# ViT tower with a top-2 mixture of experts: three of eight late shared blocks worked in halves between the routed units, and the low halves of the rows made on VectorE

## The chip, the cores and the metric

One core of one Trainium2 chip (trn2) runs the kernel. The metric is the device time of one execution in microseconds (us), all stages included. Engines are named as in the profile: PE is TensorE, DVE VectorE, ACT ScalarE, POOL GpSimd, SP SyncE, whose queue issues most transfers.

## What is computed

64 images of 3x224x224 become 197 tokens each of width 192. The reference, cut to what matters (x is the layer-normed h where the last line calls the feed-forward part):

```
h = tokens(images)                          # 16x16 patches, real FFT, projection
h = h + causal_conv(layernorm(h))           # a kernel of 512 taps for each channel
probs = softmax(x @ router_w); gates, idx = top_k(probs, 2)      # 8 experts
expert_out = (silu(x @ w_gate[e]) * (x @ w_up[e])) @ w_down[e]   # 192 -> 192 -> 192
routed = sum of the two chosen experts, by gate
shared = (silu(x @ ws_gate) * (x @ ws_up)) @ ws_down             # 192 -> 768 -> 192
alpha  = sigmoid(x @ sg_w + sg_b)
h = h + alpha * shared + (1 - alpha) * routed
```

## The kernel before

The program runs in stages with a barrier between each two: `embed` (tokens), `mix` (the convolution), then three stages of the feed-forward part, which the change touches. All products of these three are made of 16-bit high and low parts, so that each product is three to five matmuls.

**Shared stage** (`shared_expert`, from 330 us). The 12608 tokens are 25 blocks of `BT` = 512 (the last has 384). A block's shared expert is `NSH` = 6 chunks of 128 hidden units; a chunk is `up` on PE (5 + 5 matmuls of 512 columns), silu on ACT (L1233), `hidden` on DVE (hf, L1492), the high part on ACT (hh, L1239), `low` on DVE (hl, L1497) and `down` on PE (12 matmuls of 192 columns, L1160), which takes chunk c - 2 after `up` of chunk c. After six chunks `token_out` (L1504) adds a block to its sums in SBUF. Only the first `NOW` = 20 blocks get their chunks here, so 120 chunks; five blocks are left for the last stage.

In the same stage all 25 blocks must be prepared and routed. One *body* p of the schedule does that for a block while `PACE[p]` chunks are worked: 5, 5, 4, again and again, and 8 in the last. For each block: `add` on DVE (hin + yin, statistics, L1353 to L1367), `rstd` on POOL (the deviations, L1284 to L1291, ends in nb), `normal` and `x_high` on ACT (L1204, L1212: the normed rows and their high halves), `x_low` on POOL (L1296, L1297: their low halves), `transposes` on PE (L1110), `x_out` on ACT, `router` on PE, `logits` and top-2 on DVE, `ranks` on PE, `read_ranks` (L1406) and `slots` (its first is gb, its last L1442) on DVE, and `send` on POOL: two indirect DMAs (L1310) for each of four tiles scatter the rows to the list of their expert in DRAM. Before the first send of a block POOL runs one tiny operation, carry (L1308).

The order is written out by hand, one program for each engine, with semaphores. In body p POOL does send 0 and 1 of block p, `rstd` of block p + 2, send 2, `x_low` of p + 2, send 3. ACT does `normal` and `x_high` of block p + 1 in the first step of body p, after silu and before the silu of the next step. `ranks` and `slots` of block p come in the second step, or in the third where the body before had only four chunks:

```
def turn(p):
    return 2 if p and PACE[p - 1] == 4 else 1
```

In the last body, the fourth step also makes the table of the units (`unit_table`, L1454 to L1484, on DVE), after which SP writes fill rows behind each expert's list (L1096).

**Routed stage** (`routed_experts`, from 776 us). The lists are worked in units of 512 rows of one expert, here 52; the first `STRAIGHT` = 48 are written out, the rest run in a loop. A unit is 15 matmuls of 512 columns (`up`, L1652) and 20 of 192 (`down`, L1668), taken one unit later; the hidden values go through silu and parts on ACT and DVE (L1783 to L1791), `meta` and `y_out` on DVE (L1772) and ACT (L1691) write the gated result into one of two buffers y, and POOL sends it in four indirect DMAs (L1726) to DRAM. `y_out` of unit i waits until the sends of unit i - 2, which used the same buffer, have landed.

**Last stage** (`finish`, from 1161 us). The chunks of the five late blocks are worked as in the shared stage, in 30 steps (L1874, L1888), while all results are loaded, summed and stored.

The prepared rows of a late block stay in a ring of `XR` = 8 buffers xt until its chunks are done.

## Time and profile before

| what | us |
|---|---|
| median of 3 runs | 1275.32 (1271.84 to 1276.77) |
| the profiled execution, its own time | 1265.87 |
| its span, first to last instruction | 1264.0 |
| mean granted TensorE clock, share of full speed | 0.944 |
| busy: PE, DVE, ACT, POOL | 1044.1, 867.9, 537.2, 648.7 |
| shared stage, from its first silu to the barrier behind it | 330 to 776 |
| routed stage | 776 to 1161 |
| last stage | 1161 to 1264 |

Times in rows are us from the start of the span. "Busy" is the union of an engine's instructions; an engine with a lower share can still be the one that the others wait for. In a timeline a row is start, duration, engine, line, operation, out<-in, and in brackets the idle time before it with what ended it; "remote" is a semaphore of a DMA.

### The profile page before, as it was taken

How to read it: one execution, taken by the hardware profiler on the slowest of the kernel's cores; microseconds unless marked ns; L12 is line 12 of the kernel's file. 1: busy time of each engine (PE TensorE's matmuls, PEld its weight loads, DVE VectorE, ACT ScalarE, POOL GpSimd, SP SyncE). 2: the span in 40 equal slices, each digit the busy share in tenths (PEclk: the TensorE clock that was granted, in tenths of full speed). 3: DMA queues.
4: the chain of work that ended last, by engine and by line, in shares of the span. 5: the costliest groups of instructions: out<-in, count | busy, mean ns of one | idle time of the engine just before them, and what ended most of it. 6: DMA issues, size and time to landing. Idle time of an engine off the chain costs nothing. (4 is left out here: it accounts for less than half of the span.)

```text
span 1264.0 us, 24364 instructions
## 1 busy us (share of the span) xinstructions
PE 1044.1 (83%) x7867; PEld 719.3 (57%) x7868; DVE 867.9 (69%) x2637; ACT 537.2 (42%) x1023; POOL 648.7 (51%) x682
## 2 busy tenths in 40 slices
PE   5978997784699998999999996877778877773997
PEld 5867886683366655656666653444444444441555
DVE  6999776322487888978878763665665656651998
ACT  1234534222455565655555532444444444431332
POOL 0134412000377776777777760566666666643543
PEclk9988999787699999999999997999999899986999
DMA  8767786867994435443333126545545455333997
GB/s 295 241 231 262 238 261 157 208 137 172 200 210 137 118 92 133 135 116 96 99 102 93 52 81 175 121 102 127 121 98 126 105 118 126 87 77 105 308 305 239
DMA packets 285967, 196.08 MB, mean 155 GB/s; under 512 B 178840, under 2 KB 264602, under 8 KB 285590
## 3 DMA queue, kind: packets, MB, share of 16 engines
q1 hardware_dynamic: 251152, 142.46, 43.7%
q0 software_dynamic: 19488, 39.17, 9.1%
q10 hardware_dynamic: 15206, 12.93, 4.0%
q8 instruction: 66, 1.08, 0.4%
q14 instruction: 55, 0.45, 0.1%
HBM read 100.52 MB, written 74.65 MB: 139 GB/s over the span
## 5 line engine op out<-in xcount | busy, mean ns | idle before, releaser
L1726 POOL DMA_INDIRECT parts<-unit_yu,unit_token x208 | 217.5, 1046 | 69.9 <-issue 62.1
L1310 POOL DMA_INDIRECT routed<-rows_w,slot x198 | 215.8, 1090 | 65.6 <-issue 65.6
L1160 PE MATMUL pso<-ffn_w_hi,hh 128*128 128x192 f16 x480 | 119.3, 248 | 23.9 <-DVE hl L1497 17.6
L1492 DVE SCALAR_TENSOR_TENSOR hf<-psu,sg 128x512 f32<-128x512 f32 x120 | 82.9, 690 | 81.2 <-ACT sg L1233 39.6
L1233 ACT ACTIVATE sg<-psg 128x512 f32<-128x512 f32 x120 | 71.9, 599 | 142.8 <-PE psg L1145 96.0
L454 POOL TENSOR_TENSOR e_rs<-e_ve,mhalf 98x8 f32<-98x8 f32 x16 | 49.8, 3113 | 139.2 <-DVE e_ve L692 132.5
L1160 PE MATMUL pso<-ffn_w_hi,hl 128*128 128x192 f16 x480 | 119.0, 248 | 0.0
L1160 PE MATMUL pso<-ffn_w_lo,hh 128*128 128x192 f16 x480 | 119.0, 248 | 0.0
L1145 PE MATMUL psg<-xt,ffn_w_hi 128*128 128x512 f16 x360 | 118.5, 384 | 0.0
L1145 PE MATMUL psu<-xt,ffn_w_hi 128*128 128x512 f16 x360 | 117.9, 382 | 0.0
L1652 PE MATMUL u_gate<-unit_xtu,ffn_w_hi 128*128 128x512 f16 x156 | 55.6, 413 | 60.8 <-issue 35.1
L524 PE MATMUL ps<-w,area 128*98 128x192 f32 x528 | 100.6, 335 | 0.0
L402 ACT ACTIVATE u<-spare,e_nb,e_rs 98x192 f32<-98x192 f32 x124 | 56.1, 535 | 92.3 <-POOL e_nb L456 73.3
L1145 PE MATMUL psg<-xt,ffn_w_lo 128*128 128x512 f16 x240 | 92.1, 384 | 0.0
L1145 PE MATMUL psu<-xt,ffn_w_lo 128*128 128x512 f16 x240 | 91.7, 382 | 0.0
L1691 ACT ACTIVATE unit_yu<-u_out,unit_gates 128x192 f32<-128x192 f32 x104 | 38.1, 417 | 125.8 <-remote 78.3
L1497 DVE TENSOR_TENSOR hl<-hf,hh 128x512 f16<-128x512 f32 x120 | 90.7, 756 | 0.3 <-ACT hh L1239 0.3
L524 PEld LDWEIGHTS ps<-w,area 128*98 128x98 f32 x528 | 83.3, 169 | 5.3
L1783 DVE SCALAR_TENSOR_TENSOR unit_h<-u_up,stage 128x512 f32<-128x512 f32 x52 | 36.0, 692 | 60.9 <-remote 21.3
L1239 ACT CAST hh<-hf 128x512 f16<-128x512 f32 x120 | 73.7, 614 | 7.1 <-DVE hf L1492 4.9
L1921 POOL TENSOR_TENSOR end_part<-end_part 128x768 f32<-128x768 f32 (+1 forms) x25 | 47.4, 1899 | 55.8 <-DMA end_part<-parts 55.8
L1668 PE MATMUL u_out<-ffn_w_hi,unit_h0h 128*128 x208 | 51.8, 249 | 25.9 <-DVE unit_yu L1772 25.9
(245 smaller groups left out, 2806.9 us busy)
## 6 DMA issues: line engine op xcount, KB each, us to landing
end_part<-parts SPq DMA_DIRECT2D x48, 384.0 KB, 5.6
area<-in_xa_dram SPq DMA_DIRECT2D x33, 392.0 KB, 5.1
area<-in_xb_dram SPq DMA_DIRECT2D x33, 392.0 KB, 6.0
resid<-spare ACTq DMA_DIRECT2D x32, 294.0 KB
hin<-resid SPq DMA_DIRECT2D x24, 384.0 KB
yin<-mixed SPq DMA_DIRECT2D x96, 96.0 KB
spare<-in_xa_dram SPq DMA_DIRECT2D x15, 392.0 KB, 6.3
spare<-in_xb_dram SPq DMA_DIRECT2D x15, 392.0 KB, 7.4
```

The costliest lines, as they stand in the source:

```text
L402: last = nc.scalar.activation(u[0:HALF, n % 2, GI * g + n // 2], h[g % NH][:, n // 2, n % 2], ACT.Identity, bias=nb[g % NH][:, n], scale=r ...
L524: nc.tensor.matmul(out, xa[(C * g + c) % NSLOT][:, t], w32[:, c], start=(plain and c == 0 and k == 0), stop=False, skip_group_check=True)
L1145: last = nc.tensor.matmul(ps[:, m % 2], wt[:, k, cols], xt[b % XR][:, x], start=(a == 0), stop=(a == 4))
L1160: last = nc.tensor.matmul(o, hx[m % 2][:, ts], wd[k][:, m], start=(a == 0 and m == 0 and t % 2 == 0), stop=(a == 2 and m == NSH - 1), skip ...
L1233: nc.scalar.activation(sg[c % 2][:], psg[:, c % 2], ACT.Silu, scale=1.0 / SCALE).then_inc(s["sg_ready"], 1)
L1239: nc.scalar.copy(hh[c % 2][:], hf[c % 2][:]).then_inc(s["hh_ready"], 1)
L1310: nc.gpsimd.indirect_dma_start(out=routed[:, :], out_offset=bass.IndirectOffsetOnAxis(ap=slot[q][:, k, t:t + 1], axis=0), in_=rows_w[q][:, ...
L1492: nc.vector.scalar_tensor_tensor(out=hf[i][:], in0=psu[:, i], scalar=1.0 / SCALE, in1=sg[i][:], op0=ALU.mult, op1=ALU.mult).then_inc(s["hf ...
L1497: nc.vector.tensor_tensor(hl[c % 2][:], hf[c % 2][:], hh[c % 2][:], ALU.subtract).then_inc(s["hl_ready"], 1)
L1652: last = nc.tensor.matmul(ps[:], w[part][:, bass.ds(col + off, 128)], x[:, c], start=(m == 0), stop=(m == 4))
L1668: last = nc.tensor.matmul(o, h[q][:, k * 128:(k + 1) * 128], w[part][:, bass.ds(col + off, D)], start=(m == 0 and k % 2 == 0), stop=(m == ...
L1726: nc.gpsimd.indirect_dma_start(out=parts[:, :], out_offset=bass.IndirectOffsetOnAxis(ap=token[q][:, k:k + 1], axis=0), in_=y[q][:, k, :], ...
```

## The change

**The tables.** Eight blocks are late (`NLATE` = 8), so that only 17 blocks get their chunks in the shared stage: 102 chunks. `PACE` is 4 for each of the 24 bodies and 6 for the last. The number of bodies, and of blocks to be prepared and routed, is as before. `turn` is not edited, but with every body at 4 it gives 2 for all bodies but the first. The ring xt gets a ninth buffer, in the SBUF of `area`.

**The guests.** Three of the eight late blocks (17 to 19) are worked in the routed stage, in halves of 256 tokens: 3 blocks x 2 halves x 6 = 36 half chunks. Units 0 to 46 take one each, but for every fourth (3, 7, ...). A half chunk is 10 matmuls of 256 columns behind the unit's `up`, and 6 of 192 behind its `down` in the next unit; one silu and one copy on ACT; `hf` and `hl` on DVE, and two additions to the sums after each sixth. The last stage keeps five blocks and its 30 steps.

**The low halves.** `x_low` leaves POOL and becomes two operations of DVE, in the second step of a body.

```diff
@@ constants
-NLATE = 5
+NLATE = 8
+HOSTED = 3
 NOW = NBLK - NLATE
-PACE = [5, 5, 4] * ((NBLK - 1) // 3) + [8]
-XR = 8
+LATE = NOW + HOSTED
+PACE = [4] * (NBLK - 1) + [6]
+XR = 9
...
+HALVES = 2 * HOSTED
+GUESTS = NSH * HALVES
+GUEST_OF = {i: n for n, i in enumerate([i for i in range(STRAIGHT - 1) if i % 4 != 3][:GUESTS])}
+HB = BT // 2
@@ shared_expert, ScalarE
                 if b >= XR:
                     act.wait_ge(s["u_ps"], NSH * (b - XR + 1))
+                if b == XR - 1:
+                    act.wait_ge(s["area_out"], 64)
@@ shared_expert, GpSimd
-            def x_low(b, nt):
-                x = xs[b % NR]
-                pool.wait_ge(s["xhi_ready"], b + 1)
-                nc.gpsimd.tensor_tensor(x[:, 0:nt, D:D + 64], xn[:, 0:nt, 128:D], x[:, 0:nt, 128:D], ALU.subtract)
-                nc.gpsimd.tensor_tensor(x[:, 0:nt, D + 64:XW], xn[:, 0:nt, 0:128], x[:, 0:nt, 0:128],
-                                        ALU.subtract).then_inc(s["xlo_ready"], 1)
...
                 send(p, 2)
-                if a < NBLK:
-                    x_low(a, tiles(a))
                 if tiles(p) == NT:
                     send(p, 3)
@@ shared_expert, VectorE
+            def x_low(b, nt):
+                x = xs[b % NR]
+                dve.wait_ge(s["xhi_ready"], b + 1)
+                nc.vector.tensor_tensor(x[:, 0:nt, D:D + 64], xn[:, 0:nt, 128:D], x[:, 0:nt, 128:D], ALU.subtract)
+                nc.vector.tensor_tensor(x[:, 0:nt, D + 64:XW], xn[:, 0:nt, 0:128], x[:, 0:nt, 0:128],
+                                        ALU.subtract).then_inc(s["xlo_ready"], 1)
...
                     if c:
                         low(c - 1)
+                    if i == 1 and r < NBLK:
+                        x_low(r, tiles(r))
                     if c % NSH == 1 and c > NSH:
                         token_out(c // NSH - 1)
@@ routed_experts, TensorE
+            def guest_up(j):
+                b, half, m = guest_place(j)
+                cols, ts = slice(m * 128, (m + 1) * 128), slice(half * HB, (half + 1) * HB)
+                if j >= 2:
+                    pe.wait_ge(late["hf_ready"], j - 1)
+                for k in range(2):
+                    prods = ((wa[0], 0), (wa[1], 0), (wa[0], 2), (wb[0], 1), (wb[1], 1))
+                    for a, (wt, x) in enumerate(prods):
+                        last = nc.tensor.matmul(gps[:, j % 2, k * HB:(k + 1) * HB], wt[:, k, cols],
+                                                t["xt"][b % XR][:, x, ts], start=(a == 0), stop=(a == 4))
+                last.then_inc(late["g_ps"], 1)
...
             def body(i, q, k, landed):
                 up(i, k, landed)
+                if guest(i) is not None:
+                    guest_up(guest(i))
                 if not (isinstance(i, int) and i == 0):
                     down(i - 1, 1 - q)
+                if isinstance(i, int) and guest(i - 1) is not None:
+                    guest_down(guest(i - 1))
@@ routed_experts, ScalarE
                 nc.scalar.copy(h1s[q][S], h1[q][S]).then_inc(s["h1h_ready"], 1)
+                j = guest(i)
+                if j is not None:
+                    act.wait_ge(late["g_ps"], j + 1)
...
+                    nc.scalar.activation(sgx[j % 2], gps[:, j % 2, 0:HB], ACT.Silu,
+                                         scale=1.0 / SCALE).then_inc(late["sg_ready"], 1)
                 if not (isinstance(i, int) and i == 0):
                     y_out(i - 1, 1 - q)
+                if j is not None:
+                    act.wait_ge(late["hf_ready"], j + 1)
...
+                    nc.scalar.copy(hhx[j % 2][:], hfx[j % 2]).then_inc(late["hh_ready"], 1)
@@ routed_experts, VectorE
+                if isinstance(i, int) and guest(i - 2) is not None:
+                    guest_out(guest(i - 2))
+                j = guest(i)
+                if j is not None:
...
+                    nc.vector.scalar_tensor_tensor(out=hfx[j % 2], in0=gps[:, j % 2, HB:2 * HB], scalar=1.0 / SCALE,
+                                                   in1=sgx[j % 2], op0=ALU.mult,
+                                                   op1=ALU.mult).then_inc(late["hf_ready"], 1)
                 if not (isinstance(i, int) and i == 0):
                     meta(i - 1, 1 - q)
                     y_out(i - 1, 1 - q)
+                if j is not None:
+                    dve.wait_ge(late["hh_ready"], j + 1)
+                    nc.vector.tensor_tensor(hlx[j % 2][:], hfx[j % 2], hhx[j % 2][:],
+                                            ALU.subtract).then_inc(late["hl_ready"], 1)
@@ finish
-        CHUNKS = NSH * NLATE
+        CHUNKS = NSH * (NLATE - HOSTED)
```

The order of the program shows three places.

DVE, shared stage, the steps two and three of a body whose `turn` is 2 (hf and hl are `hidden` and `low`; rank and base are `read_ranks`). Before, in body 3, which follows a body of four:

```order
L1492 SCALAR_TENSOR_TENSOR hf<-psu,sg 128x512
L1497 TENSOR_TENSOR hl<-hf,hh 128x512
L1492 SCALAR_TENSOR_TENSOR hf<-psu,sg 128x512
L1406 TENSOR_TENSOR rank<-psx,base 128x32
L1409 TENSOR_TENSOR base<-base,psx 128x8
L1497 TENSOR_TENSOR hl<-hf,hh 128x512
L1417 TENSOR_SCALAR gb<-th 128x8
```

Now, in body 2, the same place, and so in all bodies but the first:

```order
L1500 SCALAR_TENSOR_TENSOR hf<-psu,sg 128x512
L1505 TENSOR_TENSOR hl<-hf,hh 128x512
L1373 TENSOR_TENSOR rows_w<-xn,rows_w 128x4x64
L1374 TENSOR_TENSOR rows_w<-xn,rows_w 128x4x128
L1500 SCALAR_TENSOR_TENSOR hf<-psu,sg 128x512
L1414 TENSOR_TENSOR rank<-psx,base 128x32
L1417 TENSOR_TENSOR base<-base,psx 128x8
L1505 TENSOR_TENSOR hl<-hf,hh 128x512
L1425 TENSOR_SCALAR gb<-th 128x8
```

Two subtractions into rows_w (`x_low` of the next block) now stand between the `hl` of the second step and the `hf` of the third, ahead of `read_ranks` and `slots`.

POOL, shared stage, one body (carry, the sends, the deviations of the block two further on). Before:

```order
L1308 TENSOR_TENSOR carry<-eps 128x1
L1310 DMA routed<-rows_w,slot 106496x196 x4
L1284 TENSOR_TENSOR ve<-mv,eps 128x4
L1288 TENSOR_TENSOR rs<-ve,mhalf 128x4
L1291 TENSOR_TENSOR nb<-nm,rs 128x4
L1310 DMA routed<-rows_w,slot 106496x196 x2
L1296 TENSOR_TENSOR rows_w<-xn,rows_w 128x4x64
L1297 TENSOR_TENSOR rows_w<-xn,rows_w 128x4x128
L1310 DMA routed<-rows_w,slot 106496x196 x2
L1308 TENSOR_TENSOR carry<-eps 128x1
```

Now:

```order
L1313 TENSOR_TENSOR carry<-eps 128x1
L1315 DMA routed<-rows_w,slot 106496x196 x4
L1296 TENSOR_TENSOR ve<-mv,eps 128x4
L1300 TENSOR_TENSOR rs<-ve,mhalf 128x4
L1303 TENSOR_TENSOR nb<-nm,rs 128x4
L1315 DMA routed<-rows_w,slot 106496x196 x4
L1313 TENSOR_TENSOR carry<-eps 128x1
```

The four sends and the deviations stand as they did; the two subtractions are gone from between the last four sends.

PE, routed stage, from the end of a unit's `up` to the start of the `down` of the unit before it (u_short is the third group of `up`, u_out is `down`). Before:

```order
L1652 MATMUL u_short<-unit_xtu,ffn_w_hi 128x512
L1652 REGISTER_ALU
L1652 MATMUL u_short<-unit_xtu,ffn_w_lo 128x512
L1613 TENSOR_LOAD units
L1613 ISA x2
L1668 ISA
L1668 MATMUL u_out<-ffn_w_hi,unit_h0h 128x192
```

Now:

```order
L1708 MATMUL guest_up<-area,ffn_w_hi 128x256 x2
L1708 MATMUL guest_up<-area,ffn_w_lo 128x256
L1708 MATMUL guest_up<-area,ffn_w_hi 128x256
L1708 MATMUL guest_up<-area,ffn_w_lo 128x256
L1708 MATMUL guest_up<-area,ffn_w_hi 128x256 x2
L1708 MATMUL guest_up<-area,ffn_w_lo 128x256
L1631 TENSOR_LOAD units
L1631 ISA x2
L1695 ISA
L1695 MATMUL u_out<-ffn_w_hi,unit_h0h 128x192
```

Ten matmuls of 256 columns (the last five stand here) come between the two; `area` is the ninth buffer of the ring.

## Rows read from the trace of the kernel before

**Rows 1.** windows of the four late stretches (stretch, us, busy of each engine, PEclk, DMA, GB/s)

```profile
330.00:739.00 409.00, 390.98 (x3324) 250.42 (x3323) 326.88 (x1291) 227.45 (x422) 296.70 (x332) 0.99 0.44 115
739.00:776.00 37.00, 28.75 (x198) 18.10 (x196) 23.25 (x79) 9.77 (x18) 11.59 (x13) 0.91 0.50 159
776.00:1161.00 385.00, 281.64 (x1821) 166.31 (x1822) 214.87 (x520) 159.02 (x312) 228.20 (x262) 0.93 0.47 106
1161.00:1264.00 103.00, 93.76 (x642) 57.06 (x640) 86.71 (x104) 32.00 (x60) 47.43 (x25) 0.96 0.90 284
```

**Rows 2.** instructions of one tile: carry, one per block (min/median/max ns)

```profile
L1308 POOL TENSOR_TENSOR carry<-eps x25: 189/190/592, 340.7 to 750.3; 128x1 f32<-128x1 f32 x25
```

**Rows 3.** chain of waits, one step in the last stage (start us, us)

```profile
1214.33 1.08 PE end_gate L1874 x5
1215.40 1.08 PE end_up L1874 x5
1216.48 0.99 PE end_out L1888 x12
```

**Rows 4.** timeline of ScalarE in body 15, which follows a body of four

```profile
592.07 1.86 ACT L1204 ACTIVATE xn<-area,nb,rs 128x192 f32<-128x192 f32 x4 [3.01 <-POOL nb L1291]
...
594.70 0.59 ACT L1233 ACTIVATE sg<-psg 128x512 f32<-128x512 f32 x1
```

**Rows 5.** timelines of VectorE and TensorE in body 15

```profile
595.32 0.69 DVE L1492 SCALAR_TENSOR_TENSOR hf<-psu,sg 128x512 f32<-128x512 f32 x1 [2.84 <-PE psu L1145]
595.93 1.35 DVE L1497 TENSOR_TENSOR hl<-hf,hh 128x512 f16<-128x512 f32 x1
...
598.32 0.68 DVE L1497 TENSOR_TENSOR hl<-hf,hh 128x512 f16<-128x512 f32 x1
...
599.99 0.17 DVE L1442 CAST slot<-slotf 128x8 uint32<-128x8 f32 x1
...
597.34 0.26 PE L1160 MATMUL pso<-ffn_w_hi,hh 128*128 128x192 f16 x1 [1.92 <-DVE hl L1497]
```

**Rows 6.** timeline of GpSimd in body 18: carry, and nb four sends later

```profile
650.66 0.19 POOL L1308 TENSOR_TENSOR carry<-eps 128x1 f32<-128x1 f32 x1 [1.90 <-DVE slot L1442]
...
657.69 0.20 POOL L1291 TENSOR_TENSOR nb<-nm,rs 128x4 f32<-128x4 f32 x1
```

**Rows 7.** timelines of GpSimd and VectorE: a send beside a sum

```profile
633.89 1.53 POOL L1310 DMA_INDIRECT routed<-rows_w,slot  x1 [0.16 <-issue]
...
633.61 0.95 DVE L1353 TENSOR_TENSOR area<-hin,yin 128x768 f32<-128x768 f32 x1
```

**Rows 8.** timeline of GpSimd, nb of block 2; instructions of L1504

```profile
352.02 0.21 POOL L1291 TENSOR_TENSOR nb<-nm,rs 128x4 f32<-128x4 f32 x1
...
L1504 DVE SCALAR_TENSOR_TENSOR spare<-pso,alpha,spare x48: 402/408/414, 404.6 to 647.5; 128x192 f32<-128x192 f32 x48
```

**Rows 9.** timelines of GpSimd and of SyncE's queue at the stage's end

```profile
750.27 0.19 POOL L1308 TENSOR_TENSOR carry<-eps 128x1 f32<-128x1 f32 x1 [4.79 <-DVE slot L1442]
...
758.09 11.32 SPq L1096 DMA_DIRECT2D routed<-stage  x8
...
776.38 0.10 POOL L1731 MEMSET unit_const<- 128x1 f32 x1 [17.72 <-POOLq L930]
```

**Rows 10.** timeline of VectorE: results of three routed units, one after another

```profile
916.22 0.74 DVE L1772 TENSOR_SCALAR unit_yu<-u_out,unit_gates 128x192 f32<-128x192 f32 x2 [2.72 <-remote]
...
921.24 0.74 DVE L1772 TENSOR_SCALAR unit_yu<-u_out,unit_gates 128x192 f32<-128x192 f32 x2
...
929.77 0.74 DVE L1772 TENSOR_SCALAR unit_yu<-u_out,unit_gates 128x192 f32<-128x192 f32 x2 [2.67 <-remote]
```

**Rows 11.** timelines of GpSimd and TensorE beside them

```profile
917.20 0.19 POOL L1722 TENSOR_TENSOR unit_carry<-unit_const 128x1 f32<-128x1 f32 x1 [2.23 <-DVE unit_yu L1772]
...
922.11 0.98 POOL L1726 DMA_INDIRECT parts<-unit_yu,unit_token  x1 [0.30 <-DVE unit_yu L1772]
...
917.15 0.25 PE L1668 MATMUL u_out<-ffn_w_hi,unit_h0h 128*128 x1 [2.00 <-DVE unit_yu L1772]
```

More of the change, by code:

```diff
@@ L900, in feed_forward @@
              + [x[:, 0:HELD * D].rearrange("p (t d) -> p t d", d=D) for x in (spare, area)]}
+        late = {name: ctx.enter_context(nc.semaphore("e_" + name)) for name in
+                ("g_ps", "u_ps", "sg_ready", "hf_ready", "hh_ready", "hl_ready", "down_ps", "out_ready")}
         shared_expert(nc, io, t, spare, area, block_stored, y_stored, weights, resid, mixed, routed, out, consts)
-        routed_experts(nc, t, weights, routed, parts)
-        finish(nc, t, weights, parts, out)
+        routed_experts(nc, t, late, weights, routed, parts)
+        finish(nc, t, late, weights, parts, out)
 def tiles(b):
@@ L1523, in _ @@
             stage_low(2)
+            x_low(0, NT)
             stage_low(3)
@@ L1558, in _, with routed_experts @@
             token_out(NOW - 1)
-def routed_experts(nc, t, weights, routed, parts):
+def routed_experts(nc, t, late, weights, routed, parts):
     with ExitStack() as ctx:
@@ L1774, in y_out, with guest_out @@
                 last.then_inc(s["y_d"], 1)
+            def guest_out(j):
+                b, half, m = guest_place(j)
+                if m < NSH - 1:
+                    return
+                dve.wait_ge(late["down_ps"], j + 1)
+                for k in range(2):
+                    at = 2 * half + k
+                    sums = sums_of(t, b, NT)[:, at]
+                    last = nc.vector.scalar_tensor_tensor(
+                        out=sums, in0=gpo[:, k * D:(k + 1) * D], scalar=t["alpha"][b % XR][:, at:at + 1], in1=sums,
+                        op0=ALU.mult, op1=ALU.add)
+                last.then_inc(late["out_ready"], 1)
             dve.sem_inc(s["begun"], 1)
@@ L1964, in _ @@
                 if c % NSH == 1 and c > NSH:
-                    token_out(NOW + c // NSH - 1)
+                    token_out(LATE + c // NSH - 1)
                 elif c >= 2:
```

73 lines of the change are left out of this document (54 added, 19 removed).

## The prediction

> **What bounds the kernel now.** I read the windows of the late stretches first, then the timelines of one body of the shared stage, then those of one pair of routed units. The windows show TensorE (PE) busy for 391 of the 409 us of the 24 bodies, and for 282 of the 385 us of the routed stage, at 0.93 of its clock there [rows 1]. So the shared stage is bound by PE, the routed stage by something else, and the change carries PE work from the first to the second. That is its plain promise. A step of chunk work is 1.08 + 1.08 + 0.99 = 3.15 us of PE [rows 3]; the 112 steps in the bodies make 353 us, which leaves (391 - 353) / 24 = 1.6 us for the transposes, router and ranks of a block.
>
> What the reader is to see next is that a body is not only PE work. Every block passes once round a ring of engines, and POOL's carry marks the turns: 25 of them from 340.7 to 750.3, so 17.07 us for a block [rows 2]. PE needs (112 / 24) x 3.15 + 1.6 = 16.3 us of that.
>
> The ring is: nb on POOL, `normal` and `x_high` on ACT, silu, `hidden`, `low`, `read_ranks` and `slots` on DVE, carry and four sends on POOL, nb. With `turn` at 2 it has no slack across bodies: `slots` of block p + 1 stands behind the silu that stands behind `normal` of block p + 2, and nb of p + 3 stands behind the sends of p + 1. Body 15 shows its first part, since it follows a body of four: ACT sat 3.01 us until nb, began `normal` at 592.07, the next silu only at 594.70 [rows 4], and `slots` ended at 599.99 + 0.17 = 600.16 [rows 5]. PE itself stood 1.92 us behind `hl` there [rows 5]. The second part is 7.23 us in body 18, from carry at 650.66 to the end of nb at 657.89 [rows 6]. Before, only one body in three has this order, and the longer bodies give the loss back.
>
> In the routed stage `y_out` waits for a DMA ("remote") at every other unit: 2.72 us at 916.22 and 2.67 us at 929.77, not at 921.24 [rows 10]. The cycle is `y_out`, four sends on POOL (917.20 to 923.09), and some 6.7 us until the buffer is free: 13.55 us for two units. PE waits for it too, 2.00 us in the same place [rows 11].
>
> **The change, part by part.**
>
> *Fewer chunks in a body.* 18 steps x 3.15 = 56.7 us of PE work leave the shared stage. PE would need 4 x 3.15 + 1.6 = 14.2 us for a block. But the ring now holds in all bodies: 600.16 - 592.07 = 8.09 us from `normal` to the end of `slots`.
>
> *`x_low` on DVE.* It stands inside this ring, ahead of `slots`. No row shows it on DVE. The nearest is `hl`, which is a subtraction of the same kinds, 0.68 us for 512 columns [rows 5]; 256 + 512 columns are 1.0 us. Below, the second start hidden under the first leaves 0.8; above, 1.35, as `hl` took beside a POOL operation [rows 5]. I take 1.0. What goes is that very clash: `hl` takes 0.68 again, so -0.67. The first part of the ring is 8.09 + 1.0 - 0.67 = 8.4 us. Queued behind `x_low` on DVE are `hidden` of the third step, `read_ranks` and `slots`; POOL waits for these, PE for the rows. On POOL the removal gives nothing to the ring: the subtractions stood behind nb, and POOL has 8.4 us there for four sends (7.23 us hold four sends and nb).
>
> *Carry to nb.* 7.23 us when nothing meets it. `add` of the next block now follows `slots` at once on DVE, and a send beside that sum took 1.53 instead of 0.97 us [rows 7]. The first send starts 0.7 us behind carry, late in a sum of 0.95, and one later send may meet a `low`: I take 0.3 us for both, bounds 0 and 2 x 0.56. The turn is 8.4 + 0.1 (slots to carry) + 7.55 = 16.05 us, bounds 15.5 and 16.8.
>
> By the Trainium skill (SBUF — State Buffer, "SBUF: two separate sides") VectorE and GpSimd share one port pair as an exclusive lock: a VectorE operation with two SBUF inputs keeps out a GpSimd operation that reads SBUF until it ends. By that rule `x_low`, `hl` and the sum of `add` can each hold a send, and the send of rows 7, begun 0.28 us into the sum, would be held 0.67 us: 1.64 against 1.53 measured, so the trace agrees. It speaks against putting `x_low` on VectorE, and is the long-turn rival below.
>
> *`token_out`.* It is 4 x 0.41 us [rows 8], 1.35 us back to back. In 8 of the 24 turns (chunks 13, 25, ... 97) it stands between `x_low` and `slots`: +10.8 us.
>
> *Sum of the bodies.* nb of block 2 ends at 352.23 [rows 8]; it waits for loads that do not change. Carry of block 1 is then 352.23 + 8.4 + 0.15 = 360.8, carry of block 24 is 360.8 + 23 x 16.05 + 10.8 = 740.7, against 750.27 [rows 9]: **-9.6 us**. The other 47 us of PE work removed become waiting of PE.
>
> *The last body.* It has two steps fewer (6.3 us). SP's fill rows, hung on the table of units, run until 758.09 + 11.32 = 769.41, and the next stage begins at 776.38 [rows 9]. They start 1.35 us earlier after carry, since no `token_out` stands there now, but still have to land. So the stage ends about 750.27 - 740.7 earlier, plus a part of the 7.0 us behind the fill rows: bounds 0 and 6.3, I take **-4.8**.
>
> *Ninth buffer.* ACT waits once for stores that were issued in the third and fourth body, and once, for block 24, for one `up` more: nothing in the ring; 0 to 2 us, taken as 0.
>
> *Guests in the routed stage.* A half chunk is half of 2.16 and half of 0.99, 1.58 us of PE, 57 us in all. PE is busy 282 / 52 = 5.4 us for a unit; two units and 1.5 guests are 10.8 + 2.4 = 13.2 of the 13.55 us of the cycle. On DVE `hf` and `hl` of 256 columns are 0.35 us each, and now and then 0.8 us of sums, against waits of 2.7 us ahead of the result that is waited for. ACT has more room (159 of 385 busy). What hides them is the time in which sends land; the margin on PE is 0.35 us a pair. Not hidden is the start, where no send is yet under way: two guests ahead of the first `down` and a part of a third, 3 us. For half-clock stretches in which PE has no rest left I add 2: **+5**, bounds 0 and 15 (a quarter of the 57).
>
> *Last stage.* The same 30 steps and transfers (DMA share 0.90 [rows 1]): 0.
>
> **Sum.** -9.6 - 4.8 + 5 = -9.4 us. The profiled execution took 1265.87, so 1256.5; that execution lies 9.4 below the median of the runs, 1275.32. I take the difference to the median: **1266 us**. A measurement of this kernel can tell about 0.5%, 6.4 us, from no change.
>
> **The rivals.**
>
> *Ring as forecast:* turn 15.8 to 16.3, 1260 to 1272 us. For it: two of the three parts were read in bodies with this order. Chance 0.55, of which 0.38 faster, 0.17 same.
>
> *Short turn:* 15.5, because `x_low` overlaps and no send is met. 23 x -0.55 = -12.6: 1253 us. For it: 7.23 was measured. Against: body 18 had no `add` at its start. 0.15, faster.
>
> *Long turn:* two of the four sends meet a DVE operation with two inputs, turn 16.8, +17: 1283 us. For it: rows 7, and the skill's rule, which is the same mechanism. Against: only one sum lies near each carry. 0.12, half same, half slower.
>
> *Guests break the cycle of the results* (the other side): DVE does `hf`, now and then the sums, and `hl` around `y_out`, and PE has 0.35 us to spare. If the result comes later than the buffer by all of the guests' DVE time, 1.2 us in each of 24 cycles, +29 for the +5 (which it contains): 1290 us, slower. It decides where the wait before `y_out` falls under 1.2 us; before it was 2.7. 0.08.
>
> *No ring:* if `slots` did not stand behind nb, PE would bind, 14.2 us a turn and `token_out` beside it: carry of block 24 at 687.4, -62.9 - 4.8 + 5: 1213 us. For it: PE's share of 391 in 409 us. Against: rows 4 and 5. 0.05, faster. The last 0.05 is for what I don't see: 0.02 faster, 0.02 same, 0.01 slower.
>
> **How the numbers follow.** Faster by over 0.5% 0.60, within 0.25, slower 0.15. The range of 1248 to 1284 us takes in the forecast, both turns and the bounds of the tail; it leaves out the guests' rival, the kernel without a ring and a part of the rest, 0.18.
>
> **What would show it.** Carry: 25 rows from 340 to 741, 16.5 us apart on the whole, mostly released by `slots`. ACT: a wait for nb in nearly every body. PE: some 2 us behind `hl` or the transposes in each body, busy share of the bodies near 0.87 and not 0.95. `x_low` near 1.0 us. Routed stage: 390 us, PE busy near 340, "remote" still ahead of every other `y_out`. Wrong it is if carry comes less than 15.3 us apart on the whole (then no ring), if carry to nb is over 8 us (port), or if "remote" is gone and the routed stage is over 400 us.

## The result, and the profile after

The changed kernel takes **1292.07 us** (median of 4 runs, 1289.18 to 1293.85), the kernel before 1276.05 us beside it (median of 4, 1271.84 to 1279.71). The ratio is 1.0124, with a 95% interval of 1.0087 to 1.0162: slower by 1.2%, where 1266 us was forecast and 1284 was the upper end.

The profiled execution took 1291.38 us (span 1289.5), close to its median. That of before, 1265.87, lies 10.2 us under its median. So the traces stand 25.5 us apart, the medians 16.0; what follows divides up the 25.5.

The windows of the changed kernel's late stretches answer to [rows 1] (shared bodies, end of the shared stage, routed stage, last stage):

```profile
330.00:739.00 409.00, 354.38 (x2980) 224.18 (x2978) 308.24 (x1288) 210.53 (x391) 253.30 (x285) 0.97 0.42 113
739.00:780.00 41.00, 22.56 (x140) 13.91 (x139) 19.33 (x74) 6.46 (x12) 11.16 (x14) 0.78 0.53 159
780.00:1180.00 400.00, 337.14 (x2393) 217.60 (x2391) 245.57 (x604) 184.69 (x384) 220.69 (x260) 0.95 0.46 100
1180.00:1289.00 109.00, 93.58 (x642) 57.35 (x642) 79.63 (x104) 31.96 (x60) 46.45 (x25) 0.94 0.84 269
```

TensorE is as busy as the forecast wanted to see it, 354 of 409 us in the bodies (0.87) and 337 in the routed stage. What is wrong is the lengths. They stand in three rows of instructions by tile: carry, the first projection of the units, and the sends of the results:

```profile
L1313 POOL TENSOR_TENSOR carry<-eps x25: 189/832/835, 338.6 to 750.6; 128x1 f32<-128x1 f32 x25
L1679 PE MATMUL u_gate<-unit_xtu,ffn_w_hi x156: 379/379/634, 778.4 to 1157.5; 128*128 128x512 f16 x156
L1793 POOL DMA_INDIRECT parts<-unit_yu,unit_token x208: 969/977/1449, 794.5 to 1176.8; - x104
```

Carry of block 24 comes at 750.6, not at 740.7 as forecast, and not earlier than before [rows 2]. In the trace of before, units began at 780.7 and the last send at 1150.1. Against before:

| piece | before | after | difference | forecast |
|---|---|---|---|---|
| start to carry of block 24 | 750.3 | 750.6 | +0.3 | -9.6 |
| carry to the first unit | 30.4 | 27.8 | -2.6 | -4.8 |
| first unit to the start of the last send | 369.4 | 398.4 | +29.0 | +5 |
| from there to the end of the span | 113.9 | 112.7 | -1.2 | 0 |
| sum | 1264.0 | 1289.5 | +25.5 | -9.4 |

The medians differ by 9.5 us less than these traces. Which piece holds these 9.5 us isn't known; if all of them are in the routed stage, its growth on the median is 19.5 us and not 29.

**The ring, and what was left out of it.** A turn is the time from one block's carry to the next one's. The timeline of GpSimd and VectorE in two turns of the changed kernel, a late one and one of the eight between blocks 6 and 14:

```profile
666.31 0.83 POOL L1313 TENSOR_TENSOR carry<-eps 128x1 f32<-128x1 f32 x1 [2.50 <-DVE slot L1450]
673.74 0.20 POOL L1303 TENSOR_TENSOR nb<-nm,rs 128x4 f32<-128x4 f32 x1
678.55 0.42 DVE L1373 TENSOR_TENSOR rows_w<-xn,rows_w 128x256 f16<-128x256 f32 x1
678.88 0.69 DVE L1374 TENSOR_TENSOR rows_w<-xn,rows_w 128x512 f16<-128x512 f32 x1
682.32 0.83 POOL L1313 TENSOR_TENSOR carry<-eps 128x1 f32<-128x1 f32 x1 [2.50 <-DVE slot L1450]
...
460.05 0.83 POOL L1313 TENSOR_TENSOR carry<-eps 128x1 f32<-128x1 f32 x1 [3.51 <-DVE slot L1450]
467.47 0.20 POOL L1303 TENSOR_TENSOR nb<-nm,rs 128x4 f32<-128x4 f32 x1
468.67 1.35 DVE L1525 SCALAR_TENSOR_TENSOR ffn_w_lo<-stage,ffn_w_hi 128x1152 f16<-128x1152 f32 x1
473.25 0.42 DVE L1373 TENSOR_TENSOR rows_w<-xn,rows_w 128x256 f16<-128x256 f32 x1
477.02 0.83 POOL L1313 TENSOR_TENSOR carry<-eps 128x1 f32<-128x1 f32 x1 [3.52 <-DVE slot L1450]
```

The first turn is 16.01 us: 7.63 from carry to the end of nb, 8.38 from there to the next carry (forecast 7.55 and 8.5, turn 16.05). x_low is two instructions, 1.02 us from start to end, and 0.94 of it until the next can start. Of the six turns with token_out ahead of slot and no row of weights, three are 17.2 to 17.3 (forecast 17.4) and the others 17.8, 18.0 and 18.5. So the ring is as forecast in the plain turns. But the second turn is 16.97, because the row of 1.35 us stands in it, the low half of a staged piece of weights (`stage_low`). Eight turns have it; the six of them without token_out are 16.97 to 17.14, 0.9 to 1.1 us over 16.05, and all eight together are 6.7 us over the forecast's turns. No term of the forecast holds it, though it stood in the kernel's own order.

**The routed stage.** From the first unit to the last, before and after:

```profile
781.00:1131.00 350.00, 273.36 (x1768) 160.43 (x1767) 207.37 (x498) 154.51 (x302) 214.75 (x245) 0.96 0.50 112
```
```profile
780.00:1158.00 378.00, 329.05 (x2343) 212.73 (x2342) 238.40 (x582) 180.18 (x374) 208.31 (x245) 0.97 0.47 103
```

The guests add 55.7 us to TensorE's busy time. Its rest falls from 76.6 to 48.9 us, and the other 28 us make the stage longer.

VectorE's results, the last matmul of TensorE's second projection ahead of two of them, and sends (timelines of VectorE, TensorE and GpSimd; before, the same cycle is [rows 10, 11]):

```profile
797.81 0.25 PE L1695 MATMUL u_out<-ffn_w_lo,unit_h1s 128*128 x1
800.72 0.74 DVE L1839 TENSOR_SCALAR unit_yu<-u_out,unit_gates 128x192 f32<-128x192 f32 x2 [1.56 <-remote]
...
926.52 0.74 DVE L1839 TENSOR_SCALAR unit_yu<-u_out,unit_gates 128x192 f32<-128x192 f32 x2
932.73 0.97 POOL L1793 DMA_INDIRECT parts<-unit_yu,unit_token  x1 [1.90 <-remote]
934.01 1.07 POOL L1793 DMA_INDIRECT parts<-unit_yu,unit_token  x1 [0.30 <-issue]
939.77 0.25 PE L1695 MATMUL u_out<-ffn_w_lo,unit_h1s 128*128 x1
943.91 0.74 DVE L1839 TENSOR_SCALAR unit_yu<-u_out,unit_gates 128x192 f32<-128x192 f32 x2 [2.37 <-remote]
```

"remote" stands ahead of 20 results, for 32.8 us in all (before 23, 43.0). The word was read as the semaphore of a DMA, here as a send that has not landed, and that reading is wrong. The result at 800.72 is that of the second unit, the first to use its buffer: in the program it waits for no send, and the label is there all the same. What it does wait for is TensorE's signal that `down` is done, and this comes late: it is recorded at 800.70, where the last matmul ended at 798.06. The result at 943.91 is alike. Its buffer's last send (934.01) landed early: sixteen signals, those of a whole send, are recorded at 937.36 to 937.49. TensorE's last matmul for it ended at 940.02, and the signal came at 943.88. In all 20 cases, and in all 23 before, the last signal on record is TensorE's, 0.02 to 0.03 us ahead of the result. (Signal times are in the packed trace and in no view of it.)

Before, the result at 916.22 [rows 10] is the same case. The last matmul of its `down` and the last of the next unit's `up`:

```profile
910.51 0.25 PE L1668 MATMUL u_out<-ffn_w_lo,unit_h1s 128*128 x1
914.77 0.38 PE L1652 MATMUL u_short<-unit_xtu,ffn_w_lo 128*128 128x512 f16 x1
```

The signal of `down` is recorded at 916.19, 5.4 us after the end, and those of the three groups of `up` at 916.26, 916.33 and 916.40, though their last matmuls had ended at 912.99, 914.07 and 915.15.

Late signals are so common that they shape the stage: those of `down` come more than 0.3 us behind their last matmul in 27 of 49 units here, by 2.9 us in the median, and in 31 of 50 before, by 5.2. The send at 932.73 waited 1.90 us for one too, since the program lets it start on a signal of TensorE. From one result of a buffer to the next the mean is 14.8 us now and 13.6 before (units 2 to 47; the pair shown, 17.4, is one of the longest). The part up to the end of the fourth send is the same, 7.2 us, and the part behind it grew from 6.5 to 7.6. So the cycle got longer, but it isn't the landing of sends that closes it.

### The profile page after: what moved, and what is told of

Its sections match the earlier page's. It is cut to its first block and busy times, and to the rows that moved or that the text cites. A ratio compares the mean times of both kernels' runs of the same rounds, so it can differ in the third digit from the quotient of the medians.

```text
span 1289.5 us, 24848 instructions
## 1 busy us (share of the span) xinstructions
PE 1057.7 (82%) x8047; PEld 740.5 (57%) x8048; DVE 872.2 (68%) x2723; ACT 543.4 (42%) x1059; POOL 593.2 (46%) x632
## 2 busy tenths in 40 slices
DMA packets 285971, 196.13 MB, mean 152 GB/s; under 512 B 178840, under 2 KB 264602, under 8 KB 285590
## 5 line engine op out<-in xcount | busy, mean ns | idle before, releaser
L1170 PE MATMUL pso<-ffn_w_hi,hh 128*128 128x192 f16 x408 | 103.4, 254 | 55.8 <-DVE hl L1505 30.1
L1500 DVE SCALAR_TENSOR_TENSOR hf<-psu,sg 128x512 f32<-128x512 f32 x102 | 70.3, 690 | 90.6 <-ACT sg L1245 58.0
L1170 PE MATMUL pso<-ffn_w_hi,hl 128*128 128x192 f16 x408 | 103.4, 253 | 0.0
L1170 PE MATMUL pso<-ffn_w_lo,hh 128*128 128x192 f16 x408 | 103.3, 253 | 0.0
L1155 PE MATMUL psg<-xt,ffn_w_hi 128*128 128x512 f16 x288 | 97.2, 393 | 0.0
L1155 PE MATMUL psu<-xt,ffn_w_hi 128*128 128x512 f16 x288 | 94.7, 383 | 0.0
L1170 PEld LDWEIGHTS pso<-ffn_w_hi,hh 128*128 128x128 f16 x408 | 40.8, 100 | 78.1 <-DVE hl L1505 43.0
L1155 PE MATMUL psg<-xt,ffn_w_lo 128*128 128x512 f16 x192 | 75.3, 392 | 0.0
L1155 PE MATMUL psu<-xt,ffn_w_lo 128*128 128x512 f16 x192 | 73.3, 382 | 0.0
L1505 DVE TENSOR_TENSOR hl<-hf,hh 128x512 f16<-128x512 f32 x102 | 69.7, 684 | 1.4 <-ACT hh L1251 1.4
```

Source lines behind the costliest of these rows:

```text
L1155: last = nc.tensor.matmul(ps[:, m % 2], wt[:, k, cols], xt[b % XR][:, x], start=(a == 0), stop=(a == 4))
L1170: last = nc.tensor.matmul(o, hx[m % 2][:, ts], wd[k][:, m], start=(a == 0 and m == 0 and t % 2 == 0), stop=(a == 2 and m == NSH - 1), skip ...
L1500: nc.vector.scalar_tensor_tensor(out=hf[i][:], in0=psu[:, i], scalar=1.0 / SCALE, in1=sg[i][:], op0=ALU.mult, op1=ALU.mult).then_inc(s["hf ...
L1505: nc.vector.tensor_tensor(hl[c % 2][:], hf[c % 2][:], hh[c % 2][:], ALU.subtract).then_inc(s["hl_ready"], 1)
```

## The experiments

The kernel before takes 1193 to 1195 us on the chips of sets 1, 2, 4 and 5 below, and 1279 on that of set 3, which alone is like the case's own. Ratios are against the kernel before on the same chip. The expectations of set 1 name times of the case's chip, which are some 83 us longer.

The expectations speak of chips where sends land early or late. The traces don't bear that out: what differs is TensorE's signals. Those of `down` are late in 27 to 34 of some 50 units in each trace of the case's chip and of set 3, and in none of any trace of the other sets. Below, the chips are told apart by that.

### Set 1: where the loss is

**Guests left out** (e1), so that three blocks lack their shared part:

```
-HALVES = 2 * HOSTED
+HALVES = 0
```

> The change, with the 36 guests left out on all engines: the shared expert's part of three blocks is missing from the sums. The routed stage took 370 us from its first matmul to its last send before the change, 399 with it. Theory A (the guests cost this on their own): the stage is back at 370 to 372 us, 28 us below the change, about 1263 us. Rival (something else of the change slows the routed stage: the longer program, the ninth buffer, the state in which the shared stage leaves the queues): the stage stays above 385 us, over 1278.

1189.81 us, ratio 0.9981 (0.9970 to 0.9991).

**Guests on TensorE alone** (e2): all their matmuls, none of their waits, and nothing of them on ScalarE and VectorE.

```
-                if j >= 2:
-                    pe.wait_ge(late["hf_ready"], j - 1)
...
-                pe.wait_ge(late["hl_ready"], j + 1)
...
-                        last = nc.tensor.matmul(gpo[:, k * D:(k + 1) * D], hx[j % 2][:, k * 128:(k + 1) * 128],
+                        last = nc.tensor.matmul(gpo[:, k * D:(k + 1) * D], t["xt"][b % XR][:, a, k * 128:(k + 1) * 128],
```

> The guests as work of TensorE alone: all their matmuls at the same places, waiting for nothing (the second projection reads a fixed tile), no silu, hidden, high, low or sums for them; three blocks' shared part is missing. Theory A1 (TensorE's time is not hidden: 57 us of it, of which about half shows): 1285 to 1292 us, as the change. Theory A2 (what costs is the chain of the results, that is the guests' operations on VectorE and ScalarE ahead of the results, while TensorE's part fits into its waits): within 5 us of the kernel without guests, about 1265.

1213.63 us, 1.0158 (1.0138 to 1.0179).

**stage_low in the last step of the body** (e3):

```
-                    if i == 0 and p and staged_at(p - 1):
-                        stage_low(staged_at(p - 1))
...
+                    if i == 3 and staged_at(p):
+                        stage_low(staged_at(p))
```

> The change, with the low half of a staged weight piece (1.35 us on VectorE) made in the last step of the body in place of the first step of the next. Theory B (it stands in the ring of the blocks in the ten turns from 443 to 617 us and makes each 0.95 us longer, which the forecast left out): carry of block 24 comes 9 to 10 us earlier, at 741, and the time is 8 to 10 us below the change, 1283. Rival (the turns of 17 us have another cause, such as the DMA of the loads or TensorE's lateness): carry stays at 750, no change of the time.

1204.92 us, 1.0101 (1.0084 to 1.0117).

**Guests behind the results of their unit** (e4), in words, since the same lines only change place:

```
 PE:   up(i); -guest_up(j);  down(i - 1); guest_down(j of i - 1); +guest_up(j)
 ACT:  +high(j of i - 1); silus and highs of the unit; -silu(j); y_out(i - 1); +silu(j); -high(j)
 DVE:  +low(j of i - 1); the unit's four; -hidden(j); meta, y_out(i - 1); +hidden(j); -low(j)
```

> The change, with each guest moved behind the results of its unit: TensorE makes its first projection after the unit's second one, ScalarE and VectorE take silu and hidden after y_out, and high and low at the start of the next unit, where they wait for TensorE anyway. Nothing is left out. Theory A2 (what stands ahead of the results costs): the routed stage falls by 15 to 25 us, total 1268 to 1277. Theory A1 (TensorE's time itself shows): no more than 5 us, 1287 to 1292.

1212.64 us, 1.0169 (1.0149 to 1.0189).

### Set 2: control, x_low, and a shorter ring (the same chip as set 1)

> The change, unaltered, beside the kernel before on the chip of this set: the control for the others. The first set ran on a chip on which the kernel before takes 1193 us and not 1276. Theory C (what the sends take to land differs between chips, the rest of the change costs the same): 1.2 to 1.8% over the kernel before. Rival: the loss belongs to the first chip, under 0.5%.

1212.72 us, 1.0171 (1.0146 to 1.0196): the change loses on this chip too, and somewhat more. This is what e1 to e4 are to be held against.

**x_low back on GpSimd** (e6), as the kernel before has it, with all the rest of the change.

> The change, with the low halves of the rows back on GpSimd, behind the third pair of sends as before. Forecast's term (1.0 us in the ring for x_low, 0.67 given back because low no longer meets it): the turns without token_out or stage_low, 16.0 us, become 15.7, carry of block 24 some 8 us earlier, the time up to 8 us below the change. Rival (the port: on GpSimd it slows the VectorE operations and is slowed by them): turns of 16.0 or more, no gain.

1210.89 us, 1.0159 (1.0132 to 1.0185), no difference from e5. Most plain turns fell from 15.9 to 16.1 only to 15.8 to 16.0; carry of block 24 came at 739.5 against 741.8. The move of x_low is worth about nothing within the change.

**A shorter ring** (e7), again in words:

```
 DVE   -x_low(r) in step 1            +x_low(r) in step 2, behind slots
 PE    -transposes(p + 1) in step 2   +in step 3, behind down
 PE    -router(p + 1) in step 3       +router(p) in step 0 of the next body, behind up
 ACT   -x_out(r) in step 2            +in step 3
 DVE   stage_low as in e3
```

> The change, with stage_low in the last step, x_low behind slots, the transposes of the next block behind the second projection of the last step, and its router behind the first projection of the next body. Theory B (ring: 7.6 us from carry to nb, 8.4 from nb to carry of which x_low is 1.0): turns of 15.0 us without token_out, 16.3 with it, carry of block 24 at 338 + 25 + 23 x 15.4 = 718 to 722, the time 25 to 30 us below the change. Rival (TensorE binds at 14.2 us plus what its records don't show): turns of 16, no more than the 9 us of stage_low.

**1183.32 us, 0.9920 (0.9894 to 0.9946)**: 29.4 us below the change and 0.8% below the kernel before.

> The kernel before, for its profile on the chip of this set. Theory C: its turns are 17.1 us as on the first chip, its unit takes 5.6 us where the sends land sooner, and no result waits for a DMA.

1193.84 us, one run, for its trace.

What the sets 1 and 2 show of the shared stage is in the rows of carry, of e3, e5 and e7 (instructions by tile, each of its own kernel):

```profile
L1313 POOL TENSOR_TENSOR carry<-eps x25: 188/830/834, 337.0 to 736.3; 128x1 f32<-128x1 f32 x25
```
```profile
L1313 POOL TENSOR_TENSOR carry<-eps x25: 188/831/833, 337.1 to 741.8; 128x1 f32<-128x1 f32 x25
```
```profile
L1313 POOL TENSOR_TENSOR carry<-eps x25: 188/291/295, 336.9 to 715.2; 128x1 f32<-128x1 f32 x25
```

These are e3, e5 and e7 in this order. With stage_low out of the ring carry of block 24 comes 5.5 us earlier than in e5 (9 to 10 were expected), and 7.6 to 10 earlier than in e1, e2 and e4 (743.9, 746.3, 744.7), which have the same shared stage. The time fell by 7.8 us. So theory B holds for the cause but not for the count: stage_low stands in eight turns and not in ten, and seven of them are 0.6 to 1.2 us shorter than in e5. In e7, which changes several places at once, the turns are those that its expectation named, 15.06 us and 16.28 with token_out; one turn of e7, on GpSimd and VectorE:

```profile
640.10 0.29 POOL L1313 TENSOR_TENSOR carry<-eps 128x1 f32<-128x1 f32 x1 [2.12 <-DVE slot L1450]
647.17 0.28 POOL L1303 TENSOR_TENSOR nb<-nm,rs 128x4 f32<-128x4 f32 x1
654.90 0.17 DVE L1450 CAST slot<-slotf 128x8 uint32<-128x8 f32 x1
654.98 0.42 DVE L1373 TENSOR_TENSOR rows_w<-xn,rows_w 128x256 f16<-128x256 f32 x1
655.15 0.29 POOL L1313 TENSOR_TENSOR carry<-eps 128x1 f32<-128x1 f32 x1 [2.29 <-DVE slot L1450]
```

x_low now stands behind slot, and carry starts at once beside it.

For the routed stage, windows from the first unit to the last send, of e8, e1, e2 and e5 in this order:

```profile
774.00:1082.00 308.00, 272.07 (x1820) 164.56 (x1820) 215.12 (x520) 158.45 (x312) 231.82 (x260) 0.96 0.58 131
```
```profile
770.00:1075.00 305.00, 272.42 (x1820) 164.88 (x1820) 215.09 (x520) 158.41 (x312) 230.33 (x260) 0.97 0.61 132
```
```profile
772.00:1101.00 329.00, 315.25 (x2396) 215.71 (x2396) 215.20 (x520) 160.78 (x312) 224.07 (x260) 0.98 0.54 123
```
```profile
768.00:1097.00 329.00, 316.64 (x2396) 217.15 (x2396) 245.86 (x604) 183.21 (x384) 227.50 (x260) 0.97 0.55 123
```

On this chip no result is released by "remote". TensorE has 36 us of rest in 308 without guests, and with them none but at the two ends (between 780 and 1070 it is busy all the time in e5). By the windows the guests add 43 to 45 us to its busy time. Of the 36 us of rest they fill only those in the middle, 20 us (e8, 790 to 1060), and the stage grows by 21 to 24. e2, which has no guest operation on VectorE and ScalarE, is as long as e5, and e4, which takes them out of the results' way, too. Theory A1 stands on this chip, and A2 falls.

### Set 3: fewer guests, and the gates of the sends (a chip with late signals)

**One block hosted** (e9) and **none** (e10), both with the ring of e7; a body that follows one of five has its ranks a step earlier, so x_low moves to step 1 and transposes and router stay in steps 2 and 3:

```
e9:  NLATE = 6, HOSTED = 1, PACE = [5, 4] * 12 + [6]
e10: NLATE = 5, HOSTED = 0, PACE = [5, 5, 4] * 8 + [8]
```

> The short ring of e7_lean with one block hosted in place of three: 12 guests, 114 steps in the shared stage, bodies of 5 and 4 by turns. Theory D (a body costs the larger of the ring, 15.1 us and 1.2 more with token_out, 15.8 on the mean, and TensorE, 3.15 us a step and 1.6; a guest costs 0.65 us where sends land soon): 4.5 steps need 15.8 us of TensorE, so the shared stage stays as long as e7_lean's, and 24 guests fewer give 16 us back: 0.978 of the kernel before, 1167 us on the chip of the first two sets. Rival (the guests are what makes the short bodies pay): 0.99 or more.

1268.53 us, 0.9915 (0.9886 to 0.9944).

> The short ring with no guest at all: the work of the kernel before (5 late blocks, bodies of 5, 5, 4), x_low on VectorE behind slots, transposes and router later. Theory D: TensorE needs 14.7 + 1.6 = 16.3 us for a body and binds; before, a turn took 16.7 us on the chip of the first two sets, so up to 10 us less: 0.992 to 1.0 of the kernel before. Rival (the ring was worth as much before as in the change): 0.975.

1280.11 us, 1.0007 (0.9978 to 1.0036).

e9 fell short of theory D (0.978) and e10 came at its upper end. Their carry rows, e9 and then e10:

```profile
L1321 POOL TENSOR_TENSOR carry<-eps x25: 189/292/299, 339.9 to 743.0; 128x1 f32<-128x1 f32 x25
```
```profile
L1321 POOL TENSOR_TENSOR carry<-eps x25: 188/291/299, 337.3 to 755.0; 128x1 f32<-128x1 f32 x25
```

Most of e9's turns go 17.9 to 18.2 and 14.6 to 15.1 by turns, 16.8 us on the mean, and not 15.8. TensorE is busy for 17.0 to 18.1 us of nearly all the long ones and for 13.2 to 14.8 of the short ones. That a body of five is bound by TensorE on its own and a body of four by the ring, so that a mean of both is no bound, is argued from this and not shown.

The two runs also price the guests on a chip with late signals, since they stand side by side on one. From the first unit to the last, e9 with 12 guests takes 367.4 us and e10 with none 357.4; up to the last send, the difference is 6.8. At 7 to 10 us for 12, the 36 of the change would cost 20 to 30 (an estimate), where its trace shows 29.

**Sends without gates** (e11):

```
-                    if k and isinstance(i, int):
-                        pool.wait_ge(s[("g_ps", "u_ps", "c_ps")[k - 1]], i + 3)
```

> The change, with the waits taken out that let the second to fourth send of a unit start only once TensorE has made the three parts of the first projection two units on. Theory E (in the change these waits, met later since a guest stands in TensorE's row, delay the sends and with them the buffer: 14 waits of 1.3 to 2.2 us in the profile of the change, 5 of 0.3 to 1.7 before): where sends land slowly 10 to 20 us below the change; where they land soon no result waits for them, no change. Rival (the sends then meet the loads of the next units and all get slower): slower than the change.

1329.55 us, 1.0411 (1.0367 to 1.0456). Theory E falls clearly, though the change itself (1.0124) was not run on this chip: the units now span 773.3 to 1190.0,

```profile
L1679 PE MATMUL u_gate<-unit_xtu,ffn_w_hi x156: 379/379/634, 773.3 to 1190.0; 128*128 128x512 f16 x156
```

417 us against 379 in the change. TensorE's signals come later still: in ten units ScalarE starts the silu of u_short 6.8 to 6.9 us after the last matmul, where it is 4.0 to 4.1 in eight units of the change. The gates that delay a send do not cost here, they save; how, no run shows.

### Sets 4 and 5: the guests taken out of the short ring (chips without late signals)

All are e7 with an edit from above: e12 with that of e1 and e14 with that of e2 (both lack the shared part of three blocks), e15 and e17 with that of e4; e13 and e16 are e7 itself.

> e7_lean with the guests left out (three blocks' shared part missing). On a chip where sends land late (the kernel before near 1279 us): the routed stage at 350 to 357 us from first to last unit, 22 to 29 below e13_lean_again. On a chip where they land early: 285, 24 below.

1164.47 us, 0.9743 (0.9720 to 0.9766).

> The kernel of e7_lean. Where sends land early 0.992 again. Where they land late, by the change's 1.0124 and the 27 to 29 us that the ring gave on the other chip: 0.990 to 0.993 of the kernel before, about 1268 us. Rival (late signals take part of the ring's gain): turns of over 15.5 us without token_out, 1.0.

1184.43 us, 0.9912 (0.9887 to 0.9937).

> e7_lean with the guests on TensorE alone (three blocks' shared part missing). Theory A1 (TensorE's time, wherever it stands, puts off the results and the gated sends behind it): within 5 us of e13_lean_again. Theory A2 (the guests' operations on VectorE and ScalarE ahead of the results): within 8 us of e12_lean_no_guests.

1184.93 us, 0.9917 (0.9892 to 0.9942).

> e7_lean with every guest behind the results of its unit, nothing left out. Where sends land late the cycle from one result to the buffer's return sets the pace, and a guest's first projection (1.1 us of TensorE) no longer stands ahead of the result: 10 to 25 us below e13_lean_again if A1 or A2 is right about what stands ahead of the results. Rival (the order doesn't count, TensorE's sum or the loads do): within 4 us. Where sends land early: no gain, as e4_guests_last.

1185.24 us, 0.9926 (0.9899 to 0.9952).

> The kernel of e7_lean. Where the kernel before takes 1276 to 1280 us: 0.990 to 0.993 of it, if the ring is worth 27 to 29 us there too. Where it takes 1193: 0.992 as twice before.

1186.60 us, 0.9932 (0.9911 to 0.9952).

> The kernel of e15, guests behind the results. Where sends land late: 10 to 25 us below e16_lean_third if what stands ahead of the results costs there, within 4 us if not. Where they land early: equal, as before.

1186.11 us, 0.9934 (0.9914 to 0.9954).

So 36 guests cost 20 us (e13 less e12), TensorE's part alone costs the same (e14), and their place doesn't matter (e15, e17). All of this holds on chips without late signals. Neither set fell on a chip of the other kind.

**x_low on VectorE in the kernel before** (e18), in the step where the change has it, and nothing else:

> The kernel before, with nothing changed but that VectorE makes the low halves, in the second step of a body. By the price found in the change (e6_xlow_pool against e5: 0.1%, within the error) it should stand within 0.4% of the kernel before. Rival (in the longer bodies it stands ahead of hidden and slots where TensorE binds, and TensorE waits 1 us more in each of 24 bodies): 1.01 to 1.02.

1186.20 us, 0.9942 (0.9921 to 0.9964): a gain of 0.6%, which neither side had named. Carry of block 24 comes at 735.7, and in e8 at 744.1. Rows of the tile `hl` of e8 and e18 (instructions by tile, min/median/max ns):

```profile
L1497 DVE TENSOR_TENSOR hl<-hf,hh x120: 675/682/1382, 340.6 to 765.7; 128x512 f16<-128x512 f32 x120
```
```profile
L1493 DVE TENSOR_TENSOR hl<-hf,hh x120: 676/681/693, 336.4 to 756.5; 128x512 f16<-128x512 f32 x120
```

The longest low is 0.69 us in place of 1.38: with x_low gone from GpSimd nothing doubles a VectorE subtraction there any more. In e8 it happened 16 times, each time beside x_low. That this is where the 7 us come from is argued, not shown.

## Why the prediction was wrong

- **What bounds (ring in all short bodies): right.** Plain turns of 16.0 to 16.1, parts of 7.6 and 8.4, TensorE at 0.87 of the bodies. e7's forecast used the same parts and met the plain turns within 0.1 us. The rivals of a short turn, a long turn and no ring are out.
- **"The turn is 16.05 us ... token_out +10.8": the sum lacked a term.** It listed what the change moves onto VectorE and token_out, and not `stage_low`, 1.35 us at the head of eight bodies. These eight turns are 6.7 us over the forecast's, of the 9.9 us by which carry of block 24 is off; e3, on another chip, gives back 5.9 us in its turns. The rest is not stage_low: 1.1 us in the turn from block 14 to 15, where GpSimd rests 1.83 us behind its first send (carry to nb is 9.0 to 9.2 us there in every trace, the kernel before included), 1.2 in the next, where ScalarE's silu at 613.19 ends a wait of 2.01 us with the label "remote", and about 1.3 in all the others.
- **x_low, "I take 1.0": right for its own rows** (0.94 to 1.02). What it exchanges for came out even: e6 puts the net at 0.1 us a turn.
- **Last body, -4.8: -2.6,** within its bounds of 0 and -6.3.
- **Guests, "+5, bounds 0 and 15", hidden by "the time in which sends land": this step failed, by 24 us in the traces.** It set 13.2 us of TensorE work for a pair of units against a cycle of 13.55 and called the rest free. Two things were wrong. First, the wait on which it counted was misread. At 916.22 [rows 10] the result waited not for a send but for TensorE, whose signal came 5.4 us after its last matmul. So the cycle of 13.55 us was not made of landing sends, and no row told whether more work of TensorE would fit into it. Second, three units of four have a guest, so a pair of units has two guests or one in alternation, and one with two needs 10.8 + 3.2 = 14.0 us, more than the cycle.
- **What the runs showed in its place.** The guests' time on TensorE is not hidden. On chips without late signals TensorE then never rests in the middle of the stage, and its matmuls are the whole cost, 20 us (e12, e13, e14). On the case's chip about half of their 56 us shows, 28, and a pair of units goes from 13.7 to 14.9 us (350.3 and 379.1 us between the first and the last unit, / 51 x 2). By the medians the term may be 19.5 us and not 29, which is still over its bound of 15.
- **The rival "guests break the cycle of the results" had the right place and the right time** (1290) **but not the mechanism:** it blamed VectorE's operations around the result and wanted "remote" gone. e2, e4, e14, e15 and e17 show no cost of these operations on chips without late signals, and "remote" is not gone. That its time fits the median, 1292.07, is partly luck: it holds the -9.6 us of the ring, which did not come, and the median holds 9.5 us less than the traces. Its chance of 0.08 was too low: a margin of 0.35 us on a pair of units was all that stood against it, and the forecast had no row of TensorE without rest in that stage.
- **Last stage, 0: -1.2.**
- **The sum:** 9.9 + 2.2 + 24.0 - 1.2 = 34.9 us between the forecast's -9.4 and the traces' +25.5. The forecast took the difference over to the median; since the profiled execution of before lay 10 us under its own, 9.5 of these don't show in the medians.

**Still open:** why TensorE's signals come late on some chips, and how guests lengthen the stage there, where TensorE still rests for 49 us. Neither guests left out, nor on TensorE alone, nor behind the results was run on such a chip, nor was the short ring with three blocks hosted (e9, with one, gains 0.8% there). e11 shows only that the order of the sends bears on it: without gates the stage is longer and the signals come later still.

## What to carry to other kernels

Once work is taken from the engine that bound a stage, list every instruction that stands on the chain left over, those that the change does not touch too: each can cost time there from then on (here 6.7 of 10.8 us in eight bodies). Idle time of an engine is free for guests only where it lies: here 20 of 36 us could be filled. Work moved into it pays nothing by itself: the whole gain lies in shortening the ring that the freed engine then waits for (29 us), and the guests give 20 back. Before you call idle time a wait for a DMA, look in the program for what the instruction waits for: a label such as "remote" is inferred, and an instruction that waits for no DMA and has the label too gives it away.

## What the runs showed of the hardware

**Chips differ in the routed stage.** The kernel before takes 1276 to 1279 us on two sets and 1193 to 1195 on four, and most of the difference is the routed stage: units from 780.7 to 1131.0 on the case's chip, from 774.4 to 1060.2 in e8, with carry of block 24 at 750.3 and 744.1. The work is the same: the traces of the change and of e5, the same kernel, both hold 285971 DMA packets. Only one chip was used twice, with the same time both times, so a difference of the hour is not ruled out.

**On the slower chips TensorE's signals arrive late.** In eight units of the changed kernel ScalarE starts the silu of u_short 4.0 to 4.1 us after the last matmul's end, and is idle for the last 1.7 to 3.8 us of it, though in the program it waits there for TensorE and VectorE and for no DMA (timelines of TensorE and ScalarE):

```profile
927.66 0.38 PE L1679 MATMUL u_short<-unit_xtu,ffn_w_lo 128*128 128x512 f16 x1
932.05 0.59 ACT L1755 ACTIVATE stage<-u_short 64x512 f32<-64x512 f32 x1 [2.34 <-remote]
```

On the chip of e5 the same pair follows in 0.17 us or less in every unit, in 0.04 us in 45 of 52:

```profile
900.73 0.38 PE L1679 MATMUL u_short<-unit_xtu,ffn_w_lo 128*128 128x512 f16 x1
901.15 0.59 ACT L1755 ACTIVATE stage<-u_short 64x512 f32<-64x512 f32 x1 [0.58 <-PE u_short L1679]
```

ScalarE has 47 waits for "remote" after 770 us in the change on the case's chip and 43 in the kernel before, none in e1, e4, e5 and e8. Several late signals come in one burst, as at 916.19 to 916.40 above. The ends of matmuls are modelled, but an error of theirs would not bring signals of groups that ended 1.1 us apart within 0.07 us of each other. The traces with late signals also record only 1123 to 1342 of the 3328 signals of landed sends, the others 3153 to 3245. What holds the signals back isn't known.

**A VectorE operation with two inputs keeps a small GpSimd operation waiting.** Carry, 0.19 us alone, is 0.83 beside the sum of `add` (0.96 us from 666.13), and ends at 667.14, 0.05 after it; in e7 it is 0.29 and ends at 655.44, 0.04 after the first instruction of x_low (654.98 + 0.42). The Trainium skill (SBUF — State Buffer, "SBUF: two separate sides") describes such a lock between a VectorE operation with two SBUF inputs and a GpSimd operation that reads SBUF; by its rule carry could not end before the VectorE operation does, and the rows agree. In the change it costs the ring at most 0.4 us a turn (carry to nb 7.63, where [rows 6] has 7.23), and the forecast had set 0.3 for such meetings, though of a send and not of carry.
